# A two-layer graph kernel: the edges' harmonics are copied to PSUM by ScalarE, and finished rows share the bank of the sums

## What is computed

```python
x = _layernorm(x + _L0_gnn_ref(edge_index, x))      # sum of scaled source rows over the edges of a node
# second layer, per edge e with source row (s: 8 scalars, v: 8 vectors of 3)
h = relu(edge_feat @ W1 + b1)
w = (h @ W2 + b2).reshape(e, 4, MUL, MUL)
sh0, sh1 = edge_sh[:, 0], edge_sh[:, 1:4]
m0 = ALPHA * (einsum('ei,eio->eo', s_e * sh0[:, None], w_000)
              + C110 * einsum('eim,em,eio->eo', v_e, sh1, w_110))
m1 = ALPHA * (einsum('ei,em,eio->eom', s_e, sh1, w_011)
              + einsum('eim,eio->eom', v_e * sh0[:, None, None], w_101))
# both are summed by dst, a small product of the node's own row is added, then _layernorm(x + ...)
```

## Time and profile before

| | |
|---|---|
| three runs | 3490.99, 3487.09, 3489.55 us; median 3489.55 |
| the profiled execution | 3488.94 us; its span from the first to the last instruction 3486.2 us |
| granted TensorE clock, mean | 0.928 |
| busy in the span | PE 2796.1 us (80%), DVE 2974.5 (85%), POOL 2464.9 (71%), ACT 1433.7 (41%) |
| the message layer's gathers | 1664, from 1312.5 us to 3447.1 us |

### The profile page before, as it was taken

The page is one execution under the profiler, slowest core; times in us unless marked ns, Lnnn a source line. Parts: engine busy times, 40 slices in busy tenths (PEclk is TensorE's granted clock), DMA queues, the critical chain, the costliest instruction groups (busy, mean ns, idle before and its releaser), DMA issues.

```text
span 3486.2 us, 55367 instructions
## 1 busy us (share of the span) xinstructions
PE 2796.1 (80%) x17493; PEld 1893.0 (54%) x17493; DVE 2974.5 (85%) x6514; ACT 1433.7 (41%) x3154; POOL 2464.9 (71%) x2520
## 2 busy tenths in 40 slices
PE   5699999999999987777777787777778777877775
PEld 4477776777777764444444454444445444444443
DVE  8788888888888865988888889889889888988987
ACT  0788888888888863211121112111212121112211
POOL 0677776777777657777777777777777777777774
PEclk9999999999999997999898898999989998999988
DMA  2200000000000021111111111111111111111112
GB/s 50 29 14 14 13 14 13 14 14 13 12 14 14 13 34 22 31 27 28 27 31 27 27 27 31 27 27 28 30 27 28 27 31 27 27 28 27 31 27 34
DMA packets 181444, 85.57 MB, mean 25 GB/s; under 512 B 124024, under 2 KB 167608, under 8 KB 181176
## 3 DMA queue, kind: packets, MB, share of 16 engines
q0 software_dynamic: 79872, 41.05, 8.0%
q1 hardware_dynamic: 101304, 41.07, 5.2%
HBM read 77.13 MB, written 4.81 MB: 24 GB/s over the span
## 4 chain that ended last, share of the span: by engine, by line
POOL 39%; issue 17%; ACT 17%; PE 14%; DVE 12%; DVEq 1%; DMA 1%; POOLq 0%; SPq 0%; ACTq 0%
POOL xg L435 39%; ACT z_sb L476 9%; ACT q_sb L476 7%; PE ps L635 4%; PE ps L648 4%; PE ps L593 3%; DVE prod_all L1062 2%; DVE stage L1231 2%; PE ps L623 1%; DVE oh L949 1%; DVE prod_all L1221 1%; PE ps L739 1%; DVE sumT_all L1085 1%; DVE lane L1058 1%; DVE z_sb L841 1%
## 5 line engine op out<-in xcount | busy, mean ns | idle before, releaser
L435 POOL DMA_INDIRECT xg<-x_table,idx x1664 | 1602.5, 963 | 562.7 <-issue 531.4
L435 POOL DMA_INDIRECT xg<-scaled_x_table,idx x832 | 854.9, 1028 | 400.7 <-issue 374.5
L739 PE MATMUL ps<-w2t,hT 128*128 128x256 f32 x3328 | 899.8, 417 | 283.9 <-DVE prod_all L1221 278.9
L739 PEld LDWEIGHTS ps<-w2t,hT 128*128 128x128 f32 x3328 | 643.2, 204 | 735.7 <-issue 640.3
L635 PE MATMUL ps<-prod_all,lane 128*128 128x363 bf16 (+1 forms) x2496 | 792.5, 320 | 51.8 <-DVE prod_all L1062 35.0
L1062 DVE TENSOR_SCALAR prod_all<-wide_lane,key 128x363 bf16<-128x363 bf16 (+1 forms) x2496 | 730.4, 316 | 27.8 <-PE ps L635 23.0
L1231 DVE TENSOR_REDUCE stage<-prod_all 128x192 f32<-128x1536 f32 x416 | 724.0, 1741 | 0.2 <-issue 0.2
L523 ACT ACTIVATE hT<-ps,b 64x512 f32<-64x512 f32 x416 | 284.4, 684 | 932.7 <-PE ps L732 928.6
L476 ACT ACTIVATE q_sb<-ps 128x363 bf16<-128x363 f32 (+1 forms) x1248 | 504.7, 543 | 94.2 <-PE ps L635 87.8
L476 ACT ACTIVATE z_sb<-ps 128x363 bf16<-128x363 f32 (+1 forms) x1248 | 504.7, 543 | 85.1 <-PE ps L635 81.8
L1215 DVE TENSOR_TENSOR prod_all<-ps,stage 128x768 f32<-128x768 f32 x416 | 397.1, 955 | 143.6 <-PE ps L739 68.7
(11 more groups left out here) (128 smaller groups left out, 1528.5 us busy)
## 6 DMA issues: line engine op xcount, KB each, us to landing
efT<-in_efT SPq DMA_DIRECT2D x104, 256.0 KB
xg<-x_table,idx POOLq DMA_INDIRECT x1664
xg<-scaled_x_table,idx POOLq DMA_INDIRECT x832
sh<-in_sh SPq DMA_DIRECT2D x104, 32.0 KB
idx<-in_src SPq DMA_DIRECT2D x156, 8.0 KB
scaled_x_table<-q_sb SPq DMA_DIRECT2D x2, 784.0 KB, 7.6
x_table<-x_sb SPq DMA_DIRECT2D x7, 224.0 KB, 4.7
out_rows<-q_sb SPq DMA_DIRECT2D x6, 224.0 KB
```

Source lines behind the costliest of these rows:

```text
L435: pool.indirect_dma_start(rows[k][:, t, :], None, table, bass.IndirectOffsetOnAxis(ap=idx[k][:, t:t + 1], axis=0),).then_inc(s_g[layer][k] ...
L739: mm = pe.matmul(ps_w[j % 2][:, t, :], hT[j % 2][:, t * P:(t + 1) * P], w2t[:].rearrange("p c o i -> p (c o i)"), start=True, stop=True)
```

## The change

1. A second PSUM area holds the four harmonics of each edge of a chunk (`ps_sh`, 128 x 64 numbers), once in bank 5 and once in bank 7. The lanes that `one_hots` reads are kept twice too, one copy beside each (`ps_mlane`).
2. ACT copies the harmonics of chunk n+1 from SBUF to PSUM (`harmonics`), behind the scalars of chunk n and in front of its third relu. The copy waits for the loads of the edges of chunk n+1 and for the messages of chunk n-1.
3. DVE's dots and both message operations read the harmonics from PSUM. The dots and the one-hots wait for the copy (`s_shp`) instead of the load.
4. Bank 7 is taken by the harmonics, so the rows of a finished block of the message layer go to bank 6, where the window sums are. PE turns the block into rows at the start of chunk `last_chunk_of(g) + 3`, DVE fetches them in that chunk behind its third group, PE's window sums of the chunk before wait for that, and DVE adds them behind the messages.

```diff
-        ps_mlane = ps[:, 5, 0:SW]
+        ps_mlane = [ps[:, 5 + 2 * b, 0:SW] for b in range(2)]
+        ps_sh = [ps[:, 5 + 2 * b, 128:128 + 4 * TPC].rearrange("p (t m) -> p t m", m=4) for b in range(2)]
-        ps_rows = ps[:, 7, 0:GB * D]
+        ps_rows = [ps[:, 7 - l, 0:GB * D] for l in range(2)]
+        rows_at = {last_chunk_of(g) + 3: g for g in range(NG - 1)}
...
+            def harmonics(n):
+                k = n % 2
+                act.wait_ge(s_edge[k], 32 * (n // 2) + 32)
+                if n >= 2:
+                    act.wait_ge(s_msg, 2 * (n - 1))
+                act.activation(ps_sh[k], sh[k][:], ACT.Copy).then_inc(s_shp, 1)
+
+            act.wait_ge(s_mlane, 2)
+            harmonics(0)
             for n in range(CHUNKS):
                 rectify(GPC * n)
                 rectify(GPC * n + 1)
                 scalars(n)
+                if n + 1 < CHUNKS:
+                    harmonics(n + 1)
                 rectify(GPC * n + 2)
                 rectify(GPC * n + 3)
...
-                    if j == 2 and at >= 1:
+                    if done is not None and j == 0:
+                        sums_to_rows(1, done, n - 1, 0)
+                    if j == (2 if done is None else 3) and at >= 1:
+                        if done is not None:
+                            pe.wait_ge(s_ld[1], done + 1)
                         sums(n - 1)
...
-                spans_of = lanes[:, -KEY0:SW - KEY0] if layer == 0 else ps_mlane
+                spans_of = lanes[:, -KEY0:SW - KEY0] if layer == 0 else ps_mlane[k]
+                if layer == 1:
+                    dve.wait_ge(s_shp, n + 1)
...
-                dve.wait_ge(s_edge[k], edges)
+                dve.wait_ge(s_shp, n + 1)
...
-                                  sh[k][:, :, 1:4].unsqueeze(2).to_broadcast([P, TPC, MUL, 3]),
+                                  ps_sh[k][:, :, 1:4].unsqueeze(2).to_broadcast([P, TPC, MUL, 3]),
...
-                                  sh[k][:, :, 0:1].to_broadcast([P, TPC, 4 * MUL]), ALU.mult).then_inc(s_msg, 1)
+                                  ps_sh[k][:, :, 0:1].to_broadcast([P, TPC, 4 * MUL]), ALU.mult).then_inc(s_msg, 1)
...
-                                  sh[k][:, :, 1:4].unsqueeze(3).to_broadcast([P, TPC, 3, MUL]),
+                                  ps_sh[k][:, :, 1:4].unsqueeze(3).to_broadcast([P, TPC, 3, MUL]),
...
+                    if done is not None and j == 2:
+                        fetch_rows(1, done, blocks_of(z_sb, done))
+                    if near_sums and j == 3 and at >= 1 and done is None:
                         add_sums(1, n - 1, bases)
                 reduce_products(n, k, GPC - 1)
                 messages(n, k)
+                if done is not None:
+                    add_sums(1, n - 1, bases)
```

More of the change, by code:

```diff
@@ L533, in scalars @@
                                xg[k][:, :, MUL:D].rearrange("p t (i m) -> p t i m", m=3), ACT.Copy).then_inc(s_scal, 1)
-            late = {last_chunk_of(g) + 4: g for g in range(NG - 1)}
+            def harmonics(n):
[6 more added lines that the diff above has]
+            harmonics(0)
+            late = {n + 1: g for n, g in rows_at.items()}
             for n in range(CHUNKS):
@@ L745, in message_rows, with chunk @@
                 return msg[n % 2][:, :, M0:M1]
-            def chunk(n, k, edges, at, sums):
+            def chunk(n, k, edges, at, sums, done=None):
                 g = GPC * n
@@ L1015, in centre @@
                     dve.tensor_tensor(z, rows, blocks_of(x_sb, g), ALU.add).then_inc(s_ld[1], 1)
+            def centre(layer, g, z):
+                cols = slice(g * GB, (g + 1) * GB)
+                if layer == 1:
                     dve.wait_ge(s_ld[1], g + 1)
@@ L1033, in normalise @@
                 for g in range(NG):
+                    fetch_rows(layer, g, blocks_of(buffer, g))
                     last = centre(layer, g, blocks_of(buffer, g))
@@ L1190, in _, with features @@
             dve.wait_ge(s_zero, 2)
-            dve.tensor_copy(ps_mlane, lane_f[:, 0:SW]).then_inc(s_mlane, 1)
-            dve.wait_ge(s_mlane, 1)
-            def features(n, k, landed, edges, first):
+            for b in range(2):
+                dve.tensor_copy(ps_mlane[b], lane_f[:, 0:SW]).then_inc(s_mlane, 1)
+            dve.wait_ge(s_mlane, 2)
+            def features(n, k, landed, first):
                 dve.wait_ge(s_g[1][k], landed)
-                dve.wait_ge(s_edge[k], edges)
+                dve.wait_ge(s_shp, n + 1)
                 if not first:
@@ L1248, in edge_chunk @@
                     one_hots(1, n)
-                features(n, k, landed, edges, first)
+                features(n, k, landed, first)
                 dve.wait_ge(s_ft, 2 * n + 2)
```

36 lines of the change are left out of this document (17 added, 19 removed).

## The result

| | before | changed |
|---|---|---|
| runs on the same chip | 3490.27 us median (3487.09 to 3492.56, 4 runs) | 3451.04 us median (3449.88 to 3451.82, 4 runs) |
| profiled execution | 3488.94, span 3486.2 | 3451.82, span 3449.9 |
| granted TensorE clock, mean | 0.928 | 0.933 |
| first gather of the message layer to the end of the last | 1312.53 to 3447.06 (2134.5 us) | 1308.07 to 3409.95 (2101.9 us) |

The ratio is 0.989, 95% interval 0.9876 to 0.9904; the medians lie 39.2 us apart.

A forecast was written before the change was run, and what follows sets the result against it. POOL's line of 1664 gathers was taken to bound the message layer, with DVE following. The terms, -31 us for freed gathers and +1 for lag at the end, took 30 off 3488.94: 3459 us, range 3452 to 3471.

The forecast's parts named there:

- (1): Message layer's gathers: reading harmonics from PSUM frees those held by DVE's two-SBUF operations; 31 of 31.7 us go.
- (2): DVE's dots and message operations: duration unchanged with one PSUM input, between -0.03 and +0.03 us each; 0.
- (3): ACT's copy ahead of the chunk's third relu: about 0.25 us, and the relu still comes in time for PE; 0.
- (4): Keeping the lanes twice: one more copy of 76 numbers ahead of the layer, under ACT's clearing of sums; 0.
- (5): Six finished blocks: DVE falls back up to 6 us more each; 0 on POOL, 1 us of lag at the end.
- The third rival: Between finished blocks: gain real, but DVE becomes the bound; 10 to 15 us given back, 3469 to 3474; chance 0.10.
- (6): POOL's 1.99 us pause and the roughly 40 us tail stay unchanged; the tail may shift 3 us either way.
- Nothing is gained: Message layer's gathers: the rival that PSUM input does not free them; 3489 us, within 0.2%; chance 0.05.
- The copy comes late in every chunk: Rival: harmonics land late, delaying DVE's third products 1.06 us in every chunk; 43 us slower, 3532; chance 0.04.
- DVE becomes the bound between the blocks: Rival: DVE's reserve runs out between finished blocks; 10 to 15 us given back, 3469 to 3474; chance 0.10.

The follow-up runs named there:

- e1: Changed kernel with ACT's copy of the harmonics going to a second SBUF tile instead of PSUM: 3481.2 us, 0.9984 of before.
- e3: Changed kernel with the dots reading the harmonics from SBUF again, both message operations still from PSUM: 3462.2 us, 0.9928 of before.
- e4: Changed kernel with both message operations reading the harmonics from SBUF again, the dots still from PSUM: 3472.1 us, 0.9959 of before.
- e6: Changed kernel with ten extra small DVE sums, 6.50 us, behind each of the six finished blocks: 3473.2 us, 0.9966 of before.
- e7: Changed kernel with one extra small DVE sum, 0.61 us, in each of the 104 chunks: 3479.8 us, 0.9985 of before.
- e5: Changed kernel run once more, unaltered: 3452.7 us, 0.9912 of before.
- e12: Kernel before run again, unaltered, to see where its first gather starts: 3487.6 us, 1.0008 of before.
- e8: Changed kernel with DVE fetching finished rows ahead of the chunk's first products and window sums back at their usual places: 3453.8 us, 0.9914 of before.
- e2: Changed kernel keeping only the new handling of finished blocks, harmonics read from SBUF, no copies on ACT: 3483.0 us, 0.9990 of before.
- set 2: Runs on one chip of e5, e6, e7 and e8, with 20 runs of the kernel before among them, median 3484.6 us.
- e9: Kernel before, unaltered, one profiled run on a chip with a low TensorE clock: 5297.7 us.
- e11: Changed kernel, unaltered, one run on the chip with a low TensorE clock: 5387.7 us.

## Why the prediction missed, step by step

The mechanism was right and the time was missed by what the sum took as unchanged. The forecast took 30 us off. Between the two profiled spans lie 36.3 us: the layer starts 4.5 us earlier, its gathers take 32.7 us less, and the tail behind them is 0.8 us longer.

**(1) The harmonics in PSUM**, -31. Right: 31.3 us of busy time went (1602.53 to 1571.23), and e1, e3 and e4 show that it was this. The mean is 944 ns, where at most 946 was forecast; the last gather ends at 3410, where 3416 was. Five gathers of over 0.98 us are left. All five start within operations of the finished blocks that read two tensors from SBUF (L1039, L1041 and L1049), and end 0.81 or 0.82 us after them; of the 560 that start within the sums of the products (L1255), which read one tensor, none is held.

**(2) The duration of the three operations**, 0. Right: L1264 and the dots take 0.55 us, where they took 0.55 and 0.54.

**(3) ACT's copy**, 0. Right in what it costs the kernel: e1, which has the copy and not its benefit, is 0.9984 of before (0.9975 to 0.9993). It takes 0.232 us, where 0.25 was forecast. But "the relu still comes in time" was wrong, and in chunks in step with their gathers, the kind that the prediction followed. This is one (timeline of the changed kernel, 1548 to 1592 us):

```profile
1571.81 0.43 SPq L354 DMA_DIRECT2D sh<-in_sh  x1
...
1574.29 0.23 ACT L544 ACTIVATE ps<-sh 128x64 f32<-128x64 f32 x1 [2.66 <-DMA sh<-in_sh]
1574.54 1.39 ACT L527 ACTIVATE hT<-ps,b 64x512 f32<-64x512 f32 x2
...
1575.28 3.02 PE L754 MATMUL ps<-w2t,hT 128*128 128x256 f32 x8 [3.63 <-ACT hT L527]
...
1578.33 0.96 DVE L1239 TENSOR_TENSOR prod_all<-ps,stage 128x768 f32<-128x768 f32 x1 [0.95 <-PE ps L754]
```

The copy starts 2.48 us after the load's issue, where 2.15 was taken from the earlier trace rows; PE's weights wait for the relu behind it, and DVE's third products wait 0.95 us. In 18 of the 36 chunks whose dots start within 2.3 us of the gathers' end the third products wait over 0.3 us for PE. Over all chunks such waits sum to 26.7 us, where they summed to 15.3 before, and PE's weights wait 113.4 us for relus in 1500 to 3400 us, a wait that was not among those of before. DVE waits for gathered rows in just these chunks, so it had the time to spare, and the kernel loses nothing. Behind a block ACT waits up to 10.9 us for a load of harmonics, which in turn stands behind DVE's messages (the 7.00 us at 1725.98 above).

**(4) Lanes twice**, 0. Nothing in the traces speaks against it.

**(5) The finished blocks**, 0 on POOL and 1 at the end. Right in kind: DVE waits 13.6 us in the block's chunk where 13 was taken (7 kept and up to 6 new). Behind the block at chunk 33 the gathers end at 2013.5, so that the rows are there 1.4 us later, and the dots run at 2030.4: 15.5 us late where 13.5 was forecast, with 4.3 us to spare where 4.5 was; behind the last block it is only 2.4. The third rival needed two sizes wrong at once: the lag was out by 2 us, the copy's 0 by some 1 us in half of the chunks in step, and e6 and e7 show how near the edge that was. At the end the dots of the last chunk run 5.5 us behind the gathers' end, 4.5 before, and the tail is 40.0 us in place of 39.1, which would be the 1 us taken. But in e5, the same kernel, these are 3.7 and 38.8, so the 1 us can't be told from scatter.

**(6) The base and what is unchanged.** Here is the step that failed. The first layer has no term in the sum, the 3488.94 of one profile was taken for the kernel's time, and "the scatter of the runs (4 us)" is the spread of three runs. From the forecast's 3458.9 to the profiled 3451.8 are 7.1 us. Its parts, each rounded:

- 4.5 us: the message layer starts at 1308.1 in place of 1312.5. Before itself has it at 1311.4 in e12, and the changed kernel and e1 to e8 have it from 1306.8 to 1313.1.
- 1.4 us: the gaps between the gathers sum to 530.6 us in place of 532.0. That too is no part of the change: e12 has 530.5.
- 0.3 us more of holds than the 31 taken, and 0.2 less of tail.
- 0.8 us outside the span of the profile: 3488.94 - 3486.2 = 2.7 us of the device time before, 3451.82 - 3449.9 = 1.9 after. This is not scatter. In the 57 runs of kernels with ACT's copy it is 1.9 to 2.2 us, in the 72 runs of the sets that go without it (before and e2) 2.4 to 3.1. The prediction had no term for it, and where it arises no profile shows.

Over the sets the median of before is 3490.3, 3487.0, 3484.6, 3484.5 and 3487.6, and in set 2 alone its runs reach from 3479.7 to 3495.8, a half width of 8 us, not 4. The gathers' stretch on the other hand repeats within half a microsecond: 2134.5 and 2134.8 before, 2101.9 and 2101.4 changed, 33 us apart. With the 0.8 us that makes some 34 us for the change. The two sets that have the changed kernel allow it: 39.2 us on 3490.3 in the first, with an interval of 33.5 to 43.3 us, and 31.9 us on 3484.6 in set 2, with 25.8 to 35.2. With 3486 as the base the sum is 3452; the medians are 3451.0 and 3452.7. The second of these lies inside the forecast's range, so that the first lies 1 us outside is chance; that both lie at its very edge is not.

What scatters is seen in the untouched first layer. The same code, 100 to 130 us after the start, before and changed (us, busy time of PE, PEld, DVE, ACT and POOL, granted clock):

```profile
100.00:130.00 30.00, 11.18 (x40) 5.55 (x41) 19.46 (x53) 21.73 (x26) 20.13 (x16) 0.78 0.25 30
```

```profile
100.00:130.00 30.00, 11.26 (x45) 5.54 (x46) 19.95 (x54) 21.95 (x27) 20.11 (x16) 1.00 0.25 30
```

Both had PE busy for 54.9 of the 100 us ahead of this. One then runs for 13.7 us at 1.2 GHz, and the other stays at 2.4. It goes with no kernel: e5, the changed kernel again, falls there too. Summed over the clock's records up to the first gather, the first profile has 69.4 us at 1.2 GHz and the changed kernel's 46.0, and e3, with 70.0, has its first gather at 1313.1 like the first profile's 1312.5. (The 105.8 and 81.9 us in the expectations of e5 and e9 are too high: they count in full a stretch of 58 us at 1.2 GHz that begins 22 us ahead of the first gather.) But e12 has its first gather at 1311.4 with 55.0 us, and e5 at 1308.4 with 62.1. So the clock may be part of it and is not all, and the cause stays open.

**The rivals.** "Nothing is gained" fell with e1, e3 and e4. "The copy comes late in every chunk" fell as a loss with e1; the delay itself is there, 0.95 us in the chunk above where the rival had 1.06, in half of the chunks in step, and DVE's waits for gathered rows covered it. "DVE becomes the bound between the blocks" did not come true here, but e6 (3473 us) and e7 (3480) are what it looks like, and on the chip of e9 to e11 DVE and PE were the bound from the start.

## What to carry to other kernels

Where POOL's indirect DMAs set the time, look for DVE operations with two SBUF inputs: each one within which a gather starts can hold it until 0.81 us after the operation's own end, and moving one small input to PSUM frees them at the price of a copy on an idle engine. Before spending slack on the engine behind the bound, sum it in both its parts, the lag after the worst chunk and the rate at which it is made up again, for the second decides whether the first adds up. And take the base from more than one profile: a stage that repeats within half a microsecond can be forecast well, and the kernel's time still be missed by the scatter of a stage that nobody touched.

## What was not expected of the hardware

On the chip of e9 to e11 the same program takes 1.52 times as long (5294.9 us of span against 3486.2), although the mean clock is only a fifth lower (0.762 against 0.928) and the single operations last about as long (L1215 956 ns in e9's groups and 955 in those of before, a matmul of the weights 444 and 417). What is different is when PE's matmuls are issued. Eight weights' matmuls that take 1.97 us together in the earlier trace rows come one by one in e9 (timeline of PE, 3060 to 3070 us):

```profile
3062.48 0.38 PE L739 MATMUL ps<-w2t,hT 128*128 128x256 f32 x1 [1.01 <-issue]
3063.89 0.38 PE L739 MATMUL ps<-w2t,hT 128*128 128x256 f32 x1 [1.03 <-issue]
3065.28 0.38 PE L739 MATMUL ps<-w2t,hT 128*128 128x256 f32 x1 [1.02 <-issue]
3067.38 0.58 PE L739 MATMUL ps<-w2t,hT 128*128 128x256 f32 x1 [1.72 <-issue]
```

They start 1.39 to 2.10 us apart, and nothing that the profile shows holds them. Beside such a spell lies one at the usual pace: from 3028 to 3055 us PE is busy for 21.9 of 27 us at a clock of 0.99, from 3060 to 3074 for 5.6 of 14 at 0.72. The mean clock alone does not tell of this. Nor is the clock shown to be the cause: 23% of e9's chain stands under "another core or an unknown queue", which the chain of before does not have. The change that wins 1% elsewhere loses 1.7% there in the one run that was made (5387.7 against 5297.7), so a verdict on a kernel should be taken for the chips it was measured on.
